# A recommender tower: GpSimd waits for landings among the last tile's gathers

## The reference

```python
e = jnp.stack([tbl_0[ids[:, 0]], ..., tbl_31[ids[:, 31]]], axis=1)
z = jnp.sum(e[:, row, :] * e[:, col, :], axis=2)          # 496 pairs
h = jnp.concatenate([z, dense_ctx], axis=1)               # 512 columns
h = jnp.maximum(h @ W_top1 + b_top1, 0.0)                 # 512 x 512
h = jnp.maximum(h @ W_top2 + b_top2, 0.0)                 # 512 x 256
y = h @ W_top3                                            # 256 x 1
```

## Time and profile before

| | us |
|---|---|
| three runs | 387.18, 390.46, 392.57 |
| median | 390.46 |
| profiled execution: span, first to last instruction | 386.4 |
| profiled execution: its own time | not given beside the span |
| PE busy | 299.7 (78%) |
| DVE busy | 248.2 (64%) |
| POOL busy | 228.5 (59%) |
| ACT busy | 145.3 (38%) |
| chain that ended last: issue / POOL / DMA / PE | 33% / 28% / 15% / 9% |

### The profile page before, as it was taken

How to read it: one execution, slowest core, us unless ns; L and a number is a source line. 1 busy time by engine, 2 the same in 40 slices (tenths; PEclk the granted TensorE clock), 3 DMA queues, 4 the chain that set the end, 5 groups by cost and what they waited for, 6 DMA issues and landing times.

```text
span 386.4 us, 7087 instructions
## 1 busy us (share of the span) xinstructions
PE 299.7 (78%) x2572; PEld 267.2 (69%) x2572; DVE 248.2 (64%) x326; ACT 145.3 (38%) x311; POOL 228.5 (59%) x250
## 2 busy tenths in 40 slices
PE   1767799886987967988676887877699786978477
PEld 1356689785887856877665886766598675867366
DVE  7699758675666666493756739464683955557541
ACT  3883543443162525244332424424243441113012
POOL 6456655566566656656665666566556656666700
PEclk9889779998999999989999998999969899899859
DMA  6670020202020202102020110202002000000000
GB/s 141 205 242 7 8 64 8 64 8 65 7 63 5 65 5 49 21 6 63 6 64 5 40 29 6 64 6 65 6 9 60 5 7 5 8 6 8 6 2 3
DMA packets 19036, 14.51 MB, mean 38 GB/s; under 512 B 9727, under 2 KB 16461, under 8 KB 19022
## 3 DMA queue, kind: packets, MB, share of 16 engines
q1 hardware_dynamic: 10284, 11.69, 9.5%
q0 software_dynamic: 7680, 1.98, 5.9%
q10 hardware_dynamic: 1058, 0.66, 0.6%
HBM read 14.24 MB, written 0.08 MB: 37 GB/s over the span
## 4 chain that ended last, share of the span: by engine, by line
issue 33%; POOL 28%; DMA 15%; PE 9%; DVE 6%; another core or an unknown queue 4%; ACT 3%; DVEq 1%; ACTq 0%; POOLq 0%
POOL emb L367 28%; DMA emb<-tbl,idx 15%; DVE emb L470 2%; PE bank L683 2%; DVE prod L489 2%; PE bank L663 2%; PE bank L692 1%; PE bank L645 1%; PE bank L780 1%; DVE prod L498 1%; ACT h1T L888 1%; ACT distance L844 1%; ACT onehot L854 1%; DMA idx<-ids 1%
## 5 line engine op out<-in xcount | busy, mean ns | idle before, releaser
L367 POOL DMA_INDIRECT emb<-tbl,idx x240 | 227.3, 947 | 138.4 <-DMA emb<-tbl,idx 73.4
L489 DVE TENSOR_TENSOR prod<-emb,bank 128x1904 f32<-128x1904 f32 (+5 forms) x51 | 94.5, 1854 | 88.3 <-DMA emb<-tbl,idx 88.3
L663 PE MATMUL bank<-ident,prod 128*128 128x128 f32 x768 | 102.8, 287 | 14.0 <-issue 8.6
L663 PEld LDWEIGHTS bank<-ident,prod 128*128 128x128 f32 x768 | 94.4, 197 | 15.9 <-issue 9.9
L683 PE MATMUL bank<-zT,w_sb 128*128 128x128 f32 x480 | 70.6, 295 | 13.6 <-ACT zT L882 12.9
L645 PE MATMUL bank<-parts,onehot 125*128 125x160 bf16 (+1 forms) x816 | 77.0, 244 | 1.4 <-issue 1.3
L683 PEld LDWEIGHTS bank<-zT,w_sb 128*128 128x128 f32 x480 | 63.6, 207 | 16.7 <-issue 14.9
L645 PEld LDWEIGHTS bank<-parts,onehot 125*128 125x128 bf16 x816 | 66.2, 106 | 12.3 <-issue 4.6
L470 DVE TENSOR_REDUCE emb<-bank 128x480 f32 (+5 forms) x96 | 52.7, 584 | 17.2 <-PE bank L645 8.8
L640 PE MATMUL bank<-far_ten,named_ten 100*128 100x480 bf16 (+1 forms) x64 | 24.8, 388 | 33.1 <-issue 24.5
L888 ACT ACTIVATE h1T<-bank,b_sb 128x128 f32<-128x128 f32 x60 | 21.5, 363 | 65.9 <-PE bank L683 26.5
(11 more groups left out here) (71 smaller groups left out, 126.5 us busy)
## 6 DMA issues: line engine op xcount, KB each, us to landing
gids<-small_ids_f SPq DMA_DIRECT2D x16, 544.0 KB
emb<-tbl,idx POOLq DMA_INDIRECT x240
w_sb<-w SPq DMA_DIRECT2D x1, 1024.0 KB
w_sb<-w SPq DMA_DIRECT2D x1, 512.0 KB
tab<-tbl SPq DMA_DIRECT2D x7, 56.0 KB
tab<-tbl SPq DMA_DIRECT2D x5, 70.0 KB
tab<-tbl ACTq DMA_DIRECT2D x5, 70.0 KB
z_last<-dense SPq DMA_DIRECT2D x16, 8.0 KB
```

Of the source, the lines that this page charges most:

```text
L367: nc.gpsimd.indirect_dma_start(emb[:, t, at:at + D], None, tables[f], bass.IndirectOffsetOnAxis(ap=idx[:, t, f:f + 1], axis=0)).then_inc(d ...
L489: return nc.vector.tensor_tensor(prod[:, at * D:(at + n * a) * D].rearrange("p (j i d) -> p j i d", j=n, d=D), strided(emb_at(t, PLACES[g] ...
L663: mm = nc.tensor.matmul(bank[:, Z_BANK + place, c * P:(c + 1) * P], v[:, d, :], ident[:], start=(d == 0), stop=(d == D - 1), is_transpose= ...
```

## The change

In the last tile too GpSimd waits for landings: behind the fifth gather (place 4) until it has landed by `landed[0][1]`, which counts group 0 of the odd tiles, and behind the tenth (place 9) until fields 8 to 10 have landed by `last_landed[0]`. Nothing else is changed; the gathers, their order and their semaphores stay.

```diff
                         place = GROUP_AT[g] + i - S
                         if t < LAST_TILE and place % RUN == RUN - 1:
                             pool.wait_ge(done, 16 * (t // 2 * n + i + 1))
+                        elif t == LAST_TILE and place == RUN - 1:
+                            pool.wait_ge(landed[0][1], 16 * (t // 2 * n + i + 1))
+                        elif t == LAST_TILE and place == 2 * RUN - 1:
+                            pool.wait_ge(last_landed[0], 16 * LAST_PIECES[0][2])
```

## The result

The changed kernel took 395.88 us (median of four runs, 394.41 to 399.33), the kernel before 391.51 (387.18 to 392.67): a ratio of 1.026, with a 95% interval from 1.016 to 1.037. I had forecast 384.5. Run again in three groups of runs, each on one chip, the changed kernel stood at 0.986, 1.004 and 1.010 of the kernel before. So the first number isn't the whole result; what follows says where each comes from, as far as it is known.

What follows compares the result with a forecast made beforehand. Until 349 us GpSimd's gathers pace the kernel, then ScalarE and TensorE are held; removing that, with the waits' 2.64 us included, gains 6.0 us: 390.46 - 6.0 = 384.5 us, range 381.5 to 391.0.

Steps and rivals of the forecast that it cites:

- the hold: Last two tiles: ScalarE idle 8.79 us until 370.55, TensorE's transposes coming singly; GpSimd's pauses were to end it.
- Rivals 1 and 2: Last tile's hold returns in third gather run (gain 3.5 us, 0.20); or outlasts last gather (loss 2.6 us, 0.14).
- rival 3: Tail: the hold goes, but TensorE runs at the lower clock, 3.0 us more; gain 3.0 us, chance 0.10.
- I take the difference in span off the median: Whole kernel: the span's gain of 6.0 us is subtracted from the median 390.46 us, giving 384.5.
- rows at 118.43: Early tile: ScalarE let go in the middle of a gather run, noted as speaking against release by GpSimd's pauses.
- what sets the end: Last tile: VectorE's last sum ends at 373.95, TensorE's turn follows at 374.1, the span ends at 380.4.
- the 2.64 us of both waits: Last tile: each added GpSimd wait costs 1.32 us, so gathers 11 to 15 move by 2.64 us.
- My row of 2.02 us for sixteen matmuls: Tail: sixteen matmuls of 128 columns took 2.02 us at TensorE's upper clock, 3.71 us at the lower.
- my guess of instructions: During gathers without a pause ScalarE and TensorE run short, most likely of their own instructions; a GpSimd pause restores them.

Runs made afterwards that it cites:

- the waits that don't wait: Kernel before plus two waits at the change's places in the last tile, with counts reached in tiles 0 and 1: 391.52 us, ratio 1.001.
- SyncE's wait: Kernel before with SyncE's load of ids, from tile 4 on, issued only when the fifth gather of the tile two before has landed: 378.31 us, ratio 0.975.

## Why the prediction was wrong

**Right, within the last tile.** Counted from its first gather, forecast, then profile after, then the profile of the rerun in the delaying condition: sixth gather 7.55, 7.54, 7.61 us; eleventh 15.15, 15.05, 15.15; circle of group 0 13.85, 13.87, 13.82; product with fields 11 and 12 18.85, 18.55, 18.83; end of the last sum 24.7, 24.45, 24.6; TensorE's turn 24.85, 24.94, 24.7; end of the span 31.15, 31.3, 31.1. That two real waits of GpSimd remove the hold is shown in the delaying condition, by the changed kernel (0.986) against the waits that don't wait (1.001) on one chip. Rivals 1 and 2 didn't occur: no profile with both waits has a hold in the last tile. Nor did rival 3 as I put it: from the turn on the end took 392.6 - 386.21 = 6.4 us. But the clock did fall, earlier, as said below.

**Wrong, the step that failed**: "I take the difference in span off the median". It assumed that all but the last tile stays as in the one profile of the kernel before, and that its hold is in every execution. Both belong to a condition that changed from one group of runs to another. In the first comparison the changed kernel was profiled in the prompt one, and its tiles 4 to 12 had late landings: its last tile began 12.0 us later, a loss that no step of mine had in it. Then the hold isn't there in the kernel before either, and what is left of the change is its cost of 1.3 us. I had no rival in which the hold simply is absent and the waits cost what they cost, though rows at 118.43 and the many runs without a hold in the middle tiles could have suggested it. My row of 2.02 us for sixteen matmuls and the rest of the tail did hold.

**Also wrong, with little effect: what sets the end.** I had the end follow from VectorE's last sum, and so from the gathers, with the 2.64 us of both waits in it. The chain of waits after says otherwise; its last links, in order of time (start, us, engine):

```profile
372.52 2.15 DVE prod L493
375.70 3.26 PE bank L667 x16
...
386.84 1.16 PE bank L784 x8
```

Behind VectorE's product with group 0 all is TensorE. The turn stood 0.49 us behind the last sum (386.21 against 384.55 + 1.17 = 385.72), because TensorE came to it then. TensorE was late by its clock: I had given it 2.0 us for the sixteen transposes of chunk 1, and asked for no more than 2.1; behind 4.20 us without a matmul they took 3.26, at a granted clock of 0.60, partly at the lower level. The views of their stretch in the profile after, and in the kernel before with SyncE's wait, where the same sixteen ran at the upper level in 2.07 us (the clock is the third number from the end):

```profile
375.70:378.96 3.26, 3.25 (x17) 3.26 (x18) 1.35 (x1) 0.00 (x0) 2.02 (x3) 0.60 0.03 3
```

```profile
360.34:362.40 2.06, 2.06 (x18) 2.06 (x19) 1.35 (x1) 0.00 (x0) 1.45 (x3) 1.00 0.05 5
```

In the six profiles with both waits they took 3.26 to 3.68 us, and layer 2 behind them 1.95 to 3.11, which is most of why their last tiles differ (31.1 to 32.8 us). In the profile after the two were 1.7 us over the 2.0 and 1.95 us of the upper level. That the sum still came out right is in part luck: VectorE's path was 0.25 us shorter than forecast, TensorE's ended half a microsecond behind it. The 1.3 us of the first wait aren't touched by this, since the transposes and layer 2 together took 5.6 to 5.7 us in all four profiles compared there.

**What stays open.** What sets the condition isn't known: it was delaying in the first profile and in the first group, prompt in the first profile after and in the other four groups, on three chips, none of them that of the first group. The chip, the time and whatever else differed between groups can't be told apart. What exactly ScalarE and TensorE lack in a hold isn't shown either; my guess of instructions was argued, not tested. The Trainium skill, "Runtime: NRT & Kernel Launch", section "Instruction fetch mechanics", has fetching mostly hidden; the prompt profiles, without any hold in straight code, agree with it, and the delaying ones neither confirm nor refute it, since no row shows a late fetch. And the 1.026 of the first comparison is more than the prompt condition explains: two later groups in it gave 1.004 and 1.010, and SyncE's wait was never run beside that comparison. Three of the four runs of the kernel before in it were those shown ahead of the prediction, so they need not have met the changed kernel's condition; one kernel against itself gave 1.001 and 1.004 here, and one changed kernel 0.996 to 1.011. Whether the rest comes from this wasn't tried.

## What to carry to other kernels

One profile is one condition: before a stall in it is priced, look whether a second profile of the same kernel has it, above all when its row names no releaser. A large transfer whose issue hangs on another engine's progress drifts against the landings that an engine waits for; tying it to a landing (one more wait on its queue) made this kernel 2.5% faster in the prompt condition, more than the change did at its best (1.4%), and nothing in the delaying one. And a wait costs what lies behind it on the path that ends last: of two equal ones the first cost 1.3 us, the second nothing where TensorE ended last and about 1.0 us where its clock was up and VectorE ended last.

## What the runs showed of the hardware

The same program on the same kind of chip was seen in a delaying and in a prompt condition, which differ over the whole trace. In the delaying one SyncE started 2.0 to 3.5 us behind TensorE's turn in most tiles of the loop, releases fell into GpSimd's pauses, and the views show idle times ended by "remote", here of the changed kernel run again:

```profile
ACT zT L886 <- remote: 21.9, 10, 4.3
```

In the prompt one the same start came 0.30 to 0.36 us behind the turn every time, and no such row exists for any engine. The traces of the delaying condition hold some 2,800 to 3,000 records of semaphore updates, those of the prompt one 6,100, so the two are easily told apart; whether the missing records and the late releases have one cause is open. The kernel before takes 390 to 392 us in both, for opposite reasons: in one it pays some 8 us for the hold in the last tile, in the other some 11 to 12 us for the late landings. By the spans of its profiles the prompt one is dearer by those 4 us (391.2 against 386.4 and 387.1); the medians don't show that, and why isn't known.

A transfer of 544 KB that was started 0.7 us ahead of a gather made that gather's landing 1.2 us late (gaps of 2.8 to 2.9 us instead of 1.6); issued at or just behind the start of the first gather of a run, whose landing nobody waits for, it cost nothing that can be seen: the gaps stayed at 1.5 to 1.8 us.
